# Attention scores and row maxima issued as four 32-column matmuls, and the products with the values in the middle of a step

## What the reference computes

```
# layer 0                                     # layer 1
h = ada_norm(x, cond)                         h = ln(x) * (1 + sc1) + sh1
q, k, v = heads(h @ wq + bq), ...             q = h @ wq.T (16 heads), k, v = h @ wk.T, h @ wv.T (4 heads)
q, k = rotary(q), rotary(k)
a = softmax(q @ k.T / sqrt(32))  # over keys  a = softmax(q @ k.T / sqrt(32))
x = x + (a @ v) @ wo + bo                     x = x + g1 * (a @ v) @ wo.T
x = x + gelu(ada_norm(x) @ w1 + b1) @ w2 + b2 x = x + g2 * (gelu(h2 @ w1.T + b1) @ w2.T + b2)
```

## Time and profile before

| | |
|---|---|
| runs | 3964.51 us median of 3 (3959.38 to 3968.36) |
| profiled execution | span 3966.3 us, first to last instruction; no other time of it is given |
| TensorE busy | 3790.3 us, 96% of the span |
| VectorE, ScalarE, GpSimd busy | 62%, 40%, 40% |
| mean granted TensorE clock | 0.976 of full |
| chain that ended last | TensorE 83%, VectorE 8%, GpSimd 3%, ScalarE 3% |

### The profile page before, as it was taken

One profiled execution on the slowest core, in us unless ns is written; L12 is line 12 of the kernel. 1 busy time (PEld: TensorE's weight loads), 2 busy tenths in 40 slices (PEclk: granted clock), 3 DMA queues, 4 the chain that ended last, 5 costly groups with the idle time before them and its releaser, 6 DMA issues.

```text
span 3966.3 us, 53519 instructions
## 1 busy us (share of the span) xinstructions
PE 3790.3 (96%) x20404; PEld 1507.3 (38%) x20404; DVE 2467.7 (62%) x3951; ACT 1601.7 (40%) x2807; POOL 1603.3 (40%) x907
## 2 busy tenths in 40 slices
PE   7988999999999999999999999999999999999999
PEld 4422444233443335432254323433244333533344
DVE  5687735766457655576654777367664776467752
ACT  1465313554125642155521663136521563126621
POOL 2466212673216632066510672136520672226611
PEclk8899999999999999999999999999999999999999
DMA  5233243212433123331233012311123112311122
GB/s 155 56 98 111 82 107 84 80 41 89 104 80 81 44 87 93 103 81 44 105 96 94 22 41 91 111 44 28 62 94 101 31 39 80 109 59 25 62 67 96
DMA packets 139021, 305.21 MB, mean 77 GB/s; under 512 B 19680, under 2 KB 59636, under 8 KB 137872
## 3 DMA queue, kind: packets, MB, share of 16 engines
q10 hardware_dynamic: 50944, 174.62, 13.6%
q1 hardware_dynamic: 87824, 127.17, 12.2%
HBM read 223.46 MB, written 36.66 MB: 66 GB/s over the span
## 4 chain that ended last, share of the span: by engine, by line
PE 83%; DVE 8%; POOL 3%; issue 3%; ACT 3%; DMA 1%; ACTq 0%; SPq 0%; POOLq 0%; DVEq 0%
PE ps L834 12%; PE ps L836 12%; PE ps L835 12%; PE ps L1014 11%; PE ps L935 9%; PE ps L997 8%; PE ps L871 7%; PE ps L1029 5%; DVE mcol L1517 3%; PE ps L888 3%; ACT probs L1194 2%; POOL sums L730 2%; DVE ring L1567 2%; PE ps L852 1%; DVE turn L1451 1%
## 5 line engine op out<-in xcount | busy, mean ns | idle before, releaser
L1517 DVE TENSOR_REDUCE mcol<-ps 128x1 f32<-128x512 f32 x2048 | 1288.5, 682 | 470.6 <-PE ps L935 470.2
L730 POOL TENSOR_TENSOR sums<-probs 128x1024 f32<-128x1024 f32 x448 | 1057.6, 2376 | 967.6 <-PE ps L1029 525.9
L1194 ACT ACTIVATE probs<-ps 128x512 f32<-128x512 f32 x2048 | 1098.2, 608 | 826.9 <-PE ps L997 592.8
L935 PE MATMUL ps<-ks,qs 97*128 97x512 f16 x2048 | 789.4, 389 | 61.3 <-DVE mcol L1517 43.6
L997 PE MATMUL ps<-qs,ks 98*128 98x512 f16 x2048 | 773.2, 387 | 72.3 <-ACT probs L1194 67.2
L1340 ACT ACTIVATE sums<-ps,cols 128x512 f32<-128x512 f32 x256 | 175.8, 687 | 1096.9 <-PE ps L836 1096.9
L1014 PE MATMUL ps<-probs,v_sb 128*32 128x512 f32 x4096 | 567.0, 628 | 0.0
L935 PEld LDWEIGHTS ps<-ks,qs 97*128 97x128 f16 x2048 | 201.2, 99 | 619.0 <-DVE mcol L1517 361.9
L834 PE MATMUL ps<-ring,probs 128*128 128x512 f16 x1024 | 388.0, 379 | 0.3 <-DVE probs L1612 0.3
L834 PE MATMUL ps<-aT,ring 128*128 128x512 f16 x1024 | 388.0, 379 | 0.0
L836 PE MATMUL ps<-aT,ring 128*128 128x512 f16 x1024 | 388.0, 379 | 0.0
(11 more groups left out here) (110 smaller groups left out, 3293.4 us busy)
## 6 DMA issues: line engine op xcount, KB each, us to landing
ring<-halves ACTq DMA_DIRECT2D x208, 512.0 KB, 3.4
qs<-hl SPq DMA_DIRECT2D x192, 128.0 KB, 4.0
ring<-halves SPq DMA_DIRECT2D x48, 512.0 KB, 6.3
ring<-in_weights ACTq DMA_DIRECT2D x39, 512.0 KB, 4.3
halves<-ring ACTq DMA_DIRECT2D x37, 512.0 KB, 2.9
ks<-hl SPq DMA_DIRECT2D x120, 128.0 KB, 4.3
dcopy<-inverses SPq DMA_DIRECT2D x56, 256.0 KB
probs<-in_x SPq DMA_DIRECT2D x8, 1024.0 KB, 8.3
```

Of the source, the lines that this page charges most:

```text
L730: pool.tensor_tensor(sums[:, m % SUM_SLOTS, :, :], prob(u - 2), prob(u), ALU.add).then_inc(sum_set[0].sem, 1)
L935: pe.matmul(bank, qs[0:K_MAX, hh, h, P * qt:P * qt + P], ks[0:K_MAX, key_set(i, hh), key_head(i, hh, h), 512 * half:512 * half + 512], sta ...
L1194: act.activation(prob(u)[:, e, :], ps[:, w % SCORE_BANKS, :], ACT.Exp).then_inc(exp_done.sem, 1)
L1517: dve.tensor_reduce(mcol[:, blk % 2, 4 * j + qt, half:half + 1], src, AX.X, ALU.max).then_inc(n_free[0], 1)
```

## The change

Scores and the maxima that `attention` issues are each issued as four matmuls: stationary columns 0 to 31, 32 to 63, 64 to 95 and 96 to 127 of the same operand, each against the same moving operand of 512 columns, each into its own 32 partitions of the same bank (`by_columns`). One semaphore increment stands on the fourth. The maxima of `forward` and of the prologue stay one matmul each. V moves from the end of the step to its middle, behind the second score and the first half of a fill and ahead of the third maximum. No wait and no DMA is added or taken away.

```
--- before.py
+++ after.py
@@ -924,7 +924,14 @@
                                            start=(c == 0), stop=(c == C - 1))
                 mm.then_inc(n_full, 1)
 
-            def max_item(key):
+            def by_columns(bank, lhs, rhs):
+
+                for q in range(4):
+                    cut = slice(32 * q, 32 * q + 32)
+                    mm = pe.matmul(bank[cut, :], lhs[:, cut], rhs, start=True, stop=True)
+                return mm
+
+            def max_operands(key):
                 _, i, blk, k = key
                 hh, qc, g = block_of(blk)
                 if k == 0:
@@ -932,9 +939,17 @@
                 bank = bank_free(key)
                 j, qt, half = max_tile(k)
                 h = 4 * g + j
-                pe.matmul(bank, qs[0:K_MAX, hh, h, P * qt:P * qt + P],
-                          ks[0:K_MAX, key_set(i, hh), key_head(i, hh, h), 512 * half:512 * half + 512],
-                          start=True, stop=True).then_inc(n_full, 1)
+                return (bank, qs[0:K_MAX, hh, h, P * qt:P * qt + P],
+                        ks[0:K_MAX, key_set(i, hh), key_head(i, hh, h), 512 * half:512 * half + 512])
+
+            def max_item(key):
+                bank, query, keys = max_operands(key)
+                pe.matmul(bank, query, keys, start=True, stop=True).then_inc(n_full, 1)
+
+            def max_in_columns(keys_):
+                for key in keys_:
+                    bank, query, keys = max_operands(key)
+                    by_columns(bank, query, keys).then_inc(n_full, 1)
 
             def stacks_ready(i, blk):
                 hh, qc, g = block_of(blk)
@@ -994,8 +1009,8 @@
                     pe.wait_ge(exp_done.sem, exp_done.at(i, w - SCORE_BANKS + 1))
                 elif i >= 1:
                     pe.wait_ge(y_read.sem, y_read.at(i - 1, 5 + bank))
-                pe.matmul(ps[:, bank, :], ks[0:K_EXP, key_set(i, hh), key_head(i, hh, h), P * kt:P * kt + P],
-                          qs[0:K_EXP, hh, h, :], start=True, stop=True).then_inc(s_mm.sem, 1)
+                by_columns(ps[:, bank, :], ks[0:K_EXP, key_set(i, hh), key_head(i, hh, h), P * kt:P * kt + P],
+                           qs[0:K_EXP, hh, h, :]).then_inc(s_mm.sem, 1)
 
             def values(i, u):
                 hh, qc, g = block_of(u // 16)
@@ -1035,22 +1050,23 @@
                     u = 2 * s
                     if s < STEPS:
                         maxima, fills = maxima_at(i, s), FILLS[i].get(s, [])
-                        some(maxima[0:1])
+                        max_in_columns(maxima[0:1])
                         score(i, 4 * s)
-                        some(maxima[1:2])
+                        max_in_columns(maxima[1:2])
                         score(i, 4 * s + 1)
                         for key in fills:
                             fill(key, 0, 6 if key[0] in "kqv" else 12)
-                        some(() if fills else maxima[2:3])
+                    if LAG <= u < UNITS + LAG:
+                        values(i, u - LAG)
+                    if s < STEPS:
+                        max_in_columns(() if fills else maxima[2:3])
                         score(i, 4 * s + 2)
                         for key in fills:
                             if key[0] in "kqv":
                                 fill(key, 6, 12)
-                        some(maxima[2:3] if fills else maxima[3:4])
+                        max_in_columns(maxima[2:3] if fills else maxima[3:4])
                         score(i, 4 * s + 3)
-                        some(maxima[3:] if fills else maxima[4:])
-                    if LAG <= u < UNITS + LAG:
-                        values(i, u - LAG)
+                        max_in_columns(maxima[3:] if fills else maxima[4:])
                     for pair in range(SUMS // 2):
                         if s == totals_step(i, pair):
                             totals(i, 2 * pair)
```

## The result

The changed kernel takes 3984.99 us (3979.51 to 3993.38, 4 runs) against 3962.99 us (3959.38 to 3968.36, 4 runs) for the kernel before on the same chip: ratio 1.0066, interval 1.0053 to 1.0079. It is slower by 22 us, about 0.7%. Forecast were 3955 us and a gain; 3984.99 lies inside the range of 3905 to 3992, in the part that the prediction had added for other mechanisms. The times here are medians over all executions; a stray one of 7643 us in copy_early and one of 6335 us in end_in_kq_copy_early move those medians by about 1 us, and the ratios leave them out.

The account below looks back on a forecast made before the run. TensorE was taken to bound the attentions. Quiet steps -9.0 and -4.7, fills +3.7, +12.9, +8 and -3.6, filled stalls -16.5 sum to -9.2 us: 3964.5 becomes 3955 us, range 3905 to 3992.

Parts of the forecast that it names:

- The matmuls themselves: Scores and maxima on TensorE: a group of four takes 0.219 us like one now, bounds 0.216 and 0.223, at most +17 us.
- Rival D: TensorE pays for the smaller pieces through issue or unhidden weight loads: net 3972 to 4046 us, chance 0.14.
- Changes of form: TensorE switching between 128-column and 32-column matmuls: 256 pairs saved at 0.23 us, 59 us possible, not taken into the forecast.
- What takes it back in quiet steps: Attention steps without fills: three chains come due, so blocks gain only 0.35 to 0.4 us; -9.0 layer 1, -4.7 layer 0.
- the second chain: Step 2 of a block: V needs `o_copy`, third in ScalarE's queue, so V is 0.73 us late.
- Stalls that V can fill: Layer 0's waits for VectorE's weight conversions: V in the middle lies inside them, -16.5 us.
- Fills: Steps with k, q or v fills: extra pairs +3.7 and +12.9 us, lost cover +8, steps 5, 8, 10 -3.6.
- + 8 (bounds 0 and 11): Layer 0's k or q fills in steps with V but no T: next maximum waits 0.95 us for VectorE, twelve times.
- Rival C: V in the middle waits longer than at the end, at place, `o_out` or VectorE ahead of rows: 3968 to 4000, chance 0.20.
- mechanism A: Main case: TensorE's saving is mostly given back to waits on other engines; 3935 to 3968 us, chance 0.50.

Follow-up runs that it names:

- copy_early: Changed kernel with ScalarE's copy of bank 4 (the products) issued two exponentials earlier; 3960.53 us, ratio 0.9999.
- end_in_kq_copy_early: Changed kernel with V at the end in steps with a k or q fill, bank 4's copy early where the step before has V in the middle; 3930.33 us.
- cols_only: Changed kernel with V back at the end of the step, scores and maxima still as four 32-column matmuls; 3954.43 us, ratio 0.9987.
- v_columns_too: kq_wo_columns with the v fills of layer 0 also as groups of four 32-column matmuls, 256 moving columns; 3907.12 us, ratio 0.9868.
- rows_late_too: kq_wo_columns with V at the end also in step 6 of a block where VectorE has no conversion; 3905.87 us, ratio 0.9868.
- end_in_fills: Changed kernel with V at the end only in steps with a k, q or v fill; 3948.69 us, ratio 0.9971.
- Middle_in_stalls: cols_only with V in the middle only in steps where VectorE converts weights; 3926.92 us, ratio 0.9917.
- end_in_2_and_6: Changed kernel with V at the end in steps 2 and 6 of each block; 3997.61 us, ratio 1.0095.
- kq_wo_columns: end_in_kq_copy_early with each k, q or v fill in one piece, and attention's k, q and output projections as four 32-column matmuls; 3911.58 us, ratio 0.9882.

## Why the prediction was wrong

**The matmuls themselves:** right. Groups stand 0.218 to 0.22 apart, with 15232 records where 3808 stood; the bounds of 0.216 and 0.223 held. Rival D is out: cols_only is faster than before. The Trainium skill's "TensorEngine Tiling", section Gotcha 2, excludes Fast Weight Load under column tiling; the loads here are 96 to 97 ns on record (98 and 99 before) and no group is longer for them. The Trainium skill's page "TensorE: Matmul & The Clock Gate", section "Wait — 56ns, not 53.3ns?", has the figure of some 62 ns for a MATMUL with hardware decode off; v_columns_too shows 27 ns, load included, so that case isn't this one. The same section of the Trainium skill gives a floor of some 25 ns from start to start for small matmuls; the 27 lie above it.

**Changes of form:** right. 0.31 and 1.00 around V became 0.22 and 0.86, and one more pair in a split fill costs 0.21 to 0.24 (steps 2 and 7 of layer 0, step 26 of layer 1). Steps 0 and 1 of layer 0, priced at two more each, grew by 0.01 and 0.22: in step 1 the waits for VectorE took in the rest. Step 6 has one more than I counted, for its rows.

**What takes it back in quiet steps:** right in mechanism and nearly in size. Forecast were 2.61, 3.47, 4.44, 3.71 and 4.33; image 5 shows 2.61, 3.47, 4.54, 3.73 and 4.31 to 4.40. Layer 1 gained 6.6 instead of 9.0. Most of what is missing is 0.1 a block in step 2 (4.54), where V came 0.85 late and not 0.73. waits for the DMA of the row maxima (`qs<-mT`) grew as well. The view of waits before (us in total, times, longest):

```profile
PEld ps L997 <- DMA qs<-mT: 4.2, 4, 1.6
PE ps L997 <- DMA qs<-mT: 3.1, 4, 1.3
```

and after:

```profile
PEld ps L931 <- DMA qs<-mT: 16.9, 17, 2.7
PE ps L931 <- DMA qs<-mT: 8.6, 11, 2.2
```

Rows come later in their step and the next step is shorter, so the transfer has less time. That is argued from these rows and not shown; rows_late_too made the rows' step 0.2 shorter in layer 1, and the waits stayed. Copy_early shows that the second chain was `o_copy`, and at the place named.

**Stalls that V can fill:** right in mechanism; that the number is near is partly luck. Forecast were 24.8 for all of layer 0 outside the fills, measured 28.2, but this sum holds a loss behind the fills that end_in_fills gives back (11.5 net, 15.1 in steps 13 and 14), so V filled stalls worth more than I counted. Middle_in_stalls and end_in_2_and_6 show it from both sides, and the mean granted clock rose from 0.976 to 0.983 in the profiled executions.

**The step that failed is "Fills", in its term "+ 8 (bounds 0 and 11)".** It counted V's lost cover only where a k or q fill of layer 0 stands in a step with V and no T, twelve places, and took some off, since "VectorE's later waits shrink for it". Measured against it:

- those twelve cost 0.98 each beyond the second pair, 11.8 in all (+3.8 on the 8 taken). The later waits did not shrink but grew, in steps 13 and 14, which the table counts outside the fills;
- layer 1's steps 13, 14 and 25 have the same shape and cost 0.94 each, 12 x 0.94 = 11.3. I priced them at a pair only. VectorE's operation there (L1460) was not read, although it stood in the trace as the one of layer 0 did;
- step 6 of layer 0 has a v fill, which needs no VectorE, but rows behind it and no T: 4 x (2.17 - 0.23) = 7.8. Of it 4 x 0.88 = 3.5 are V's lost cover, which rows_late_too gives back (0.89 each), 2.9 the second score's longer wait for ScalarE and 1.3 the pair for the rows. I worked out rows behind V only for steps with T;
- what is left of the fills, 13.8, stands against the 72 pairs priced at 16.6.

11.3 + 7.8 + 3.8 - 2.8 = 20.1 us, which is 44.7 - 24.6. The second miss is 8.1 us of terms that I had at nothing without a reason (output projection +3.8, modulation +3.2, start +1.1; the last block balances); kq_wo_columns takes back 2.3 of the first, the rest stays open. Rival C had the sign and the size of the answer, but not the place: its `o_copy` wait exists at the price forecast, while the time came from the fills. That the measured time lies in the range is no credit to mechanism A, which ended at 3968. End_in_fills shows the cause by taking it away: -36 us for one condition.

## What to carry to other kernels

When work moves to an earlier place, list for every kind of step what the moved work covered there, not only for the kind in which you first see it: here 28 rare steps lost about 27 us of cover, and the steps behind them some 11 more, where the 268 quiet ones gained 7.5. Look for engines' stalls that the moved work can fill, and put it there alone. A saving on the bounding engine is worth little until the handoffs that it makes due are moved as well; here the change cost 22 us; with one copy placed earlier and V kept late where it is cover it gained 31, and with the fills in 32 columns as well 59.

## What the runs showed of the hardware

- Four fp16 matmuls of 32 columns into four quarters of a bank run as one of 128: 0.218 us a group with 512 moving columns, and 1.31 / 12 = 0.109 with 256. That is 27 ns for each matmul and its load, half of the 55.8 that I had used as the bound of issue. As 256 moving columns take 0.109, 128 would take 0.055 (an estimate), so that row was paced by its moving columns and said nothing of issue.
- Once TensorE had been busy 0.20 of 2.00 us, the next 4.00 us ran at a granted clock of 0.57. Where V filled part of such a wait (1.07 us idle instead of 1.87), the granted clock behind it stayed at 1.00, and T is on record with 1.03 us instead of 1.83.
